# The second attention stage: the second lane eight phases behind the first, and without its filler products

## What is computed

```python
def local_attn(q, k, v):          # windows of 128 rows, each sees itself and the one before
    dots = einsum('bwie,bwje->bwij', bq, bk2) * e ** (-0.5)
    dots = where(causal_mask | pad_mask, mask_value, dots)
    return einsum('bwij,bwje->bwie', softmax(dots), bv2)
def causal_linear_attn(q, k, v):  # buckets of 64 rows
    q, k = softmax(q), elu(k) + 1.0
    ctx = cumsum(einsum('bhund,bhune->bhude', bk, bv)) / (k_cum[..., None] + 1e-6)
    return einsum('bhund,bhude->bhune', bq, ctx_of_the_buckets_before)
x = x + self_attention(layer_norm(x)); x = x + gelu(layer_norm(x) @ W1 + b1) @ W2 + b2   # four times
```

## Time and profile before

| | |
|---|---|
| time, median of 3 runs | 5479.9 us (5474.39 to 5488.4) |
| the profiled execution, its own time | 5487.05 us |
| its span, first to last instruction | 5485.7 us |
| the stage, 1230.5 to 2464.7 us | 1234.2 us |
| PE busy in the stage | 1023.2 us |
| DVE, ACT, POOL busy in the stage | 661.0, 439.2, 148.2 us |
| mean granted clock of TensorE, whole span | 0.783 |

### The profile page before, as it was taken

The page is one execution under the profiler, slowest core; times in us unless marked ns, Lnnn a source line. Parts: engine busy times, 40 slices in busy tenths (PEclk is TensorE's granted clock), DMA queues, the critical chain, the costliest instruction groups (busy, mean ns, idle before and its releaser), DMA issues.

```text
span 5485.7 us, 96739 instructions
## 1 busy us (share of the span) xinstructions
PE 4046.9 (74%) x40667; PEld 3139.4 (57%) x40732; DVE 2918.3 (53%) x7893; ACT 1911.6 (35%) x4228; POOL 885.0 (16%) x664
## 2 busy tenths in 40 slices
PE   5786958367888888882757768586888888885398
PEld 4664848255556565552646556475555655565277
DVE  4545464425555545547255665646666666665232
ACT  3233232123333333330232332424555555552122
POOL 0000000231111101112600000002222211220534
PEclk7555565588999999985766666668999999997699
DMA  9200000150000000001210000000000000000255
GB/s 270 60 2 1 2 1 2 61 164 1 1 1 1 1 1 1 1 5 35 31 42 1 1 1 2 0 2 2 1 1 1 1 1 1 1 1 18 90 159 140
DMA packets 140868, 152.46 MB, mean 28 GB/s; under 512 B 7808, under 2 KB 128002, under 8 KB 139792
## 3 DMA queue, kind: packets, MB, share of 16 engines
q1 hardware_dynamic: 119024, 128.21, 7.9%
q0 software_dynamic: 21408, 18.05, 1.9%
HBM read 87.38 MB, written 59.76 MB: 27 GB/s over the span
## 4 chain that ended last, share of the span: by engine, by line
PE 29%; DVE 11%; ACT 7%; issue 2%; another core or an unknown queue 1%; POOL 0%; DMA 0%; SPq 0%; DVEq 0%; ACTq 0%; POOLq 0%
PE banks_lane L3108 3%; PE banks_lane L3719 3%; ACT work L3276 2%; PE banks_lane L3198 2%; PE banks_lane L810 2%; PE banks_lane L3155 2%; PE banks_lane L3185 2%; PE banks_lane L425 1%; DVE work L2822 1%; PE banks_lane L3172 1%; PE banks_lane L3212 1%; PE banks_lane L3712 1%; PE banks_lane L818 1%; PE banks_lane L2676 1%; PE banks_lane L2688 1%
## 5 line engine op out<-in xcount | busy, mean ns | idle before, releaser
L425 PE MATMUL banks_lane<-constants,work 128*128 128x128 f32 x968 | 186.3, 335 | 406.5 <-DVE work L411 161.2
L425 PEld LDWEIGHTS banks_lane<-constants,work 128*128 128x128 f32 x968 | 140.6, 173 | 476.4 <-DVE work L411 153.6
L405 POOL TENSOR_TENSOR weights<-weights,constants 128x4 f32<-128x4 f32 x76 | 78.5, 1033 | 1911.8 <-DVE weights L400 1911.8
L425 PE MATMUL banks_lane<-constants,weights 128*128 128x128 f32 x596 | 124.6, 345 | 349.8 <-DVE weights L411 94.3
L425 PEld LDWEIGHTS banks_lane<-constants,weights 128*128 128x128 f32 x596 | 88.2, 178 | 384.0 <-issue 160.6
L3276 ACT ACTIVATE work<-banks_lane,weights 128x192 f32<-128x192 f32 (+1 forms) x512 | 248.9, 505 | 134.7 <-DVE weights L3376 134.6
L405 POOL TENSOR_TENSOR work<-work,constants 128x4 f32<-128x4 f32 x76 | 77.3, 1018 | 1114.5 <-DVE work L400 1114.5
L3383 POOL TENSOR_TENSOR weights<-weights,constants 128x16 f32<-128x16 f32 x64 | 185.4, 2897 | 264.8 <-DVE weights L3288 264.8
L3198 PE MATMUL banks_lane<-constants,work 128*128 128x128 f32 x896 | 137.8, 300 | 88.6 <-ACT weights L3245 45.4
L2054 DVE TENSOR_REDUCE work<-banks_lane 128x2 f32<-128x512 f32 x256 | 158.8, 684 | 79.8 <-PE banks_lane L1915 79.6
L3372 DVE TENSOR_REDUCE weights<-banks_lane 128x2 f32<-128x384 f32 (+1 forms) x256 | 122.4, 520 | 139.9 <-PE banks_lane L3185 139.7
(11 more groups left out here) (790 smaller groups left out, 11144.4 us busy)
## 6 DMA issues: line engine op xcount, KB each, us to landing
work<-experts_dram_l_ffn SPq DMA_DIRECT2D x39, 964.0 KB
room_l_ffn<-work SPq DMA_DIRECT2D x30, 1188.0 KB, 14.1
work<-experts_dram_l_ffn SPq DMA_DIRECT2D x23, 512.0 KB
weights<-weights_dram SPq DMA_DIRECT2D x1, 4833.5 KB, 14.4
work<-room_l_ffn SPq DMA_DIRECT2D x36, 132.0 KB
weights<-weights_dram SPq DMA_DIRECT2D x1, 4112.0 KB, 12.8
weights<-bands_dram SPq DMA_DIRECT2D x1, 4096.0 KB, 13.7
weights<-room_l_ffn SPq DMA_DIRECT2D x26, 132.0 KB
```

The costliest lines, as they stand in the source:

```text
L405: pool.tensor_tensor(n.rstd, n.rstd, c("neghalf", cols=(0, n.rstd.shape[1])), ALU.pow).then_inc(*u.pool.step(name))
L425: done = pe.transpose(bank[0:rows, t * P:(t + 1) * P], block, c("ident"))
```

## The change

The stage is woven with `lead=8` in place of `lead=1`: the first eight phases of lane 0's first unit run alone, then A8 B0, A9 B1 and so on to A15 B7, A0 B8 (of lane 0's next unit), and the last eight phases of lane 1 run alone at the end. Both filler counts become 0. No other instruction is added or taken out by the text of the kernel; the order in which the engines meet them changes, and with it the places of the table loads.

```diff
--- before.py
+++ after.py
@@ -1757,7 +1757,8 @@
-L1_ATTN_NORM_FILL, L1_ATTN_SCORE_FILL = 14, 2
+L1_ATTN_NORM_FILL, L1_ATTN_SCORE_FILL = 0, 0
+L1_ATTN_LEAD = 8
@@ -2168,7 +2169,7 @@
     layers, whole = L1Attn(run, w, X, Y, lanes, enter), Unit(run, "l1_edges", 0)
     layers.start_dve(run.dve, whole)
     run.meet_all()
-    in_two_lanes(layers, run, units_of(run, [("l1_layer", n) for n in range(L1_ATTN_LAYERS)]))
+    in_two_lanes(layers, run, units_of(run, [("l1_layer", n) for n in range(L1_ATTN_LAYERS)]), lead=L1_ATTN_LEAD)
```

## The result

The changed kernel takes 5534.59 us (median of 3 runs, 5534.14 to 5542.35) against 5479.9 us before: a ratio of 1.0106, 95% interval 1.0084 to 1.0127. It is slower by 1.1%. The forecast was 5540.

What follows compares the result with a forecast made beforehand. PE (TensorE) bounds the stage, waiting on DVE. 15.5 periods of 78 us (71.8 plus 6 for the clock) plus 62 for the ends, less 1208 now, gave +63 us, so 5540; likeliest 5510 to 5575, full range 5430 to 5620.

Steps and rivals of the forecast that it cites:

- The fillers' removal: Taking 288 filler products, 4 us of PE time per pair, out of the stage was costed at nothing.
- The walk: One period of the new order, slot by slot: 54 us PE work plus 17.8 idle, 71.8 per pair at full clock.
- for the maxima: Phase 3, PE waits for the maxima of the scores from DVE: 2.8 us for lane 0, 3.1 for lane 1.
- for the rows: Phase 13, PE waits for DVE's scaled rows: 4.0 us idle for lane 0, 3.2 for lane 1.
- The clock: Half clock on TensorE behind long waits costs 6 us per pair in the new order, 4.2 in the old.
- The ends: Eight phases running alone at each end of the stage: 62 us together, between bounds of 38 and 75.
- The table loads: 32 more ACT loads of 1283 ns, as Gelu falls between exponentials, costed at nothing; 41 us if all exposed.
- The sum: Stage change: 15.5 periods of 78 us plus 62 for the ends, less 16 old pairs of 75.5: +63 us.
- 16 x 75.5: The old order's stage in the sum, 16 pairs of 75.5 us each, 1208 us.
- P: Time of one pair of units in the old order, from one project phase to the next: 75.5 us.
- The faster case: Rival: dense phases of the other lane hold 2.4 GHz, pair 71.8 us, ends 54, total 5439; chance 0.25.

Runs made afterwards that it cites:

- experiment 1: Kernel before (lead 1) with both filler counts set to 0: 5478.11 us, ratio 1.0015 to the kernel before.
- experiment 4: Changed kernel (lead 8) plus 11 filler products in each of a pair's four long waits: 5420.85 us, ratio 0.9898; rerun 5414.02 us, 0.99.
- experiment 6: Kernel before (lead 1, its 14 and 2 fillers) plus 5 fillers behind lane 0's sums and 9 ahead of lane 1's rows: 5450.49 us, ratio 0.9971.
- experiment 10: Changed kernel (lead 8) plus 11 fillers in each of the two waits for the maxima, none for the rows: 5486.02 us, ratio 1.0026.
- experiment 8: Changed kernel (lead 8) plus 22 fillers behind each unit's down products, none in the gaps: 5643.59 us.
- experiment 3: Changed kernel with lead 256 in place of 8, so one lane runs after the other, no fillers: 6231.23 us.
- experiment 5: Changed kernel with Identity in place of Gelu, so only one table load is left in the stage: 5525.13 us, ratio 1.0103.
- experiment 2: Changed kernel (lead 8) with the old 14 and 2 fillers put back where they were: 5558.88 us, ratio 1.0161.

## Why the prediction was right, point by point

- *The fillers' removal costs nothing by itself.* Right within what can be told (experiment 1), and it gave nothing back either: PE was busy for 984.1 us of that stage in place of 1023.2, but the time stayed. It is so at lead 1; at lead 8 the old fillers, in the wrong places, cost time (1.0161 with them, 1.0106 without).
- *The walk: 71.8 us for a pair at full clock, 0.5 more than now.* With the clock held a pair took 71.4 us, and 71.6 in the old order (experiments 4 and 6). The long waits came where they were walked: for the maxima 2.66 us (lane 0) and 2.69 (lane 1), walked at 2.8 and 3.1; for the rows 3.14 (lane 0) and 2.75 (lane 1), walked at 4.0 and 3.2. Lane 0's is shorter because the work beside it ran at half clock: in experiment 10, where that work runs at full clock, it is 3.97 us. Part of the agreement is luck. In the pair of experiment 4, 64.9 us of PE less 9.7 of filler leave 55.2 of own work and 16.2 of waits, forecast at 54 and 17.8, two errors that nearly cancel. And the terms written down for the maxima (3.45, 1.6, 1.85 and 1.0 out of 10.2 to 10.6) leave 2.3 to 2.7 us for lane 0 and, without the 1.6, 3.9 to 4.3 for lane 1, not 2.8 and 3.1; in lane 1's case the turns of phase 11 and short waits lie in that time as well.
- *The clock: 6 us for a pair, 4.2 now.* It measured 78.5 - 71.4 = 7.1 us, and for now 75.5 - 71.6 = 3.9. The stretches of 6.7 and 3.3 us at 0.50 shown above go with such waits. The prediction found its trace in agreement with the rule on idle gaps that it cites (the Trainium skill, TensorE: Matmul & The Clock Gate, HAM oscillation); the waits that cost the clock here, of 2.66 to 3.14 us, are shorter than the idle gaps that the rule names, so their price is shown by the runs and not by the rule. That it is the clock, and not the waits as such, is shown by experiment 4, in which the waits stay and only what PE does in them changes, and by experiment 8, in which the same products stand elsewhere.
- *The ends: 62 us.* A unit alone takes 61.4 us (experiment 3). In the changed kernel the ends come to more: 1281.2 - 15.5 x 78.1 = 71 us.
- *The table loads: nothing.* Right (experiment 5). The Trainium skill (ScalarE: Activation LUTs, Table sets: the hidden batching unit) asks for all functions of one set before the next. Breaking that rule 32 times more had no price here, where ACT is busy for 474 of 1284.5 us.
- *The sum, +63 us.* The stage grew by 50.3. In the three parts of the windows above, the sum had +2.5 us for the first pair, 14 x 2.5 = +35 for the next 14, and +25.5 behind them (half a period of 39 and the ends of 62, against a pair of 75.5). Measured are -10.8, +30.6 and +30.1. The term that was mis-sized is the one of now, 16 x 75.5: I had measured P on the last ten pairs, and the first one is 89.8 us long in the kernel before, at a clock of 0.85, and 79.0 in the changed one. That is the 13 us of the error; the other two differences nearly cancel. Why the old order starts so slowly was not tested. That the total came within 5.4 us of 5540 is in part luck: the medians differ by 54.7 us, the two profiled spans by 47.1.
- *The rivals.* The faster case needed a clock cost under 2 us; it was 7.1. With the gaps filled the new order goes beyond the 5439 of that case, to 5414 to 5421 us, but by the fillers: at full clock its pair is no shorter than that of the old order.

What stays open, besides the old order at full clock, is how much the removal of the fillers costs at lead 1. One execution shows a stage longer by 18.6 us, the runs a ratio of 1.0015 with 1 just inside its interval; the rest of the kernel varies by as much from one execution to the next.

## What to carry to other kernels

When lanes in a fixed order are shifted against each other, walk one period of the new order through every engine's queue: what counts is not which phases share a slot, but what stands in TensorE's list between the two ends of each long chain through VectorE. Then price the waits twice, once as idle time and once as the clock that is lost behind them; here the pairs lost by the second alone. Price the ends too: a lane that is eight phases behind ran alone at the end, and of the 50 us that was 30. Fillers are worth what they fill: they have to move when the order moves, and in their new places they turned a loss of 1.1% into a gain of 1.0%. That gain is theirs and not the order's.

## What the runs showed of the hardware that I had not expected

- Four waits of some 2.7 to 3.1 us in 78.5 us cost 7.1 us more than their own idle time. With products in them the granted clock was 1.00 over 14 pairs, though one wait of 1.55 us and one with 1.49 us left idle remain in a pair.
- The effect of fillers is not proportional: 5 in each gap held 0.95 and 11 held 0.99, from 0.87 with none. With 5, the same waits stand in every pair, and yet two of the fifteen took 71.4 us at 1.00 and the others 73.0 to 75.6 at less.
- Half clock came in stretches that began before a wait was over: at 1828.8 us, 0.7 us ahead of the end of a wait of 2.69.
- 4 us of products on the path of TensorE (experiment 2) left the period at 78.5 us, while the clock rose from 0.87 to 0.93.
